# Output transposes moved one step later in the attention loop, uneven first tiles, and a regrouped layer norm in the expert stage

## What is computed

```
# attention, layer 0 (layer 1: relu projections, no bias, no time bias, no output projection)
scores = einsum('bhqd,bhkd->bhqk', Q, K) / 4          # 16 heads of 16
attn   = softmax(scores - 0.1*|t_q - t_k|)
x      = x + tanh(g) * (einsum('bhqk,bhkd->bhqd', attn, V) @ Wo.T + bo)
# feed-forward, layer 1: each row goes through the one of 4 experts that its router picks
h = gelu(x_n @ W1[e] + b1[e])                          # 256 -> 1024
y = h @ Wo + bo + x_n                                  # 1024 -> 256
y = (y - mean) * rsqrt(var + 1e-12) * gamma + beta     # over the 256 columns
x = x + tanh(g) * y
```

## Time and profile before

| | us |
|---|---|
| median of 3 runs | 765.55 |
| lowest, highest | 762.64, 770.63 |
| the profiled execution | 768.56 |
| its span, first to last instruction | 766.8 |

### The profile page before, as it was taken

How to read it: one execution, slowest core, us unless ns; L and a number is a source line. 1 busy time by engine, 2 the same in 40 slices (tenths; PEclk the granted TensorE clock), 3 DMA queues, 4 the chain that set the end, 5 groups by cost and what they waited for, 6 DMA issues and landing times.

```text
span 766.8 us, 12504 instructions
## 1 busy us (share of the span) xinstructions
PE 704.1 (92%) x4252; PEld 422.1 (55%) x4252; DVE 583.8 (76%) x1130; ACT 451.3 (59%) x968; POOL 311.2 (41%) x369
## 2 busy tenths in 40 slices
PE   6878999999999898899998999999999899999991
PEld 3434344444443566597763444444444488998981
DVE  5565899999992369455886989999997667777775
ACT  2322788888888453765414888888888234333330
POOL 4212455555554232863520020656662543443322
PEclk9998999999999999999999999999999899999997
DMA  7788645554554514102144256422301331211100
GB/s 224 213 241 192 196 151 179 190 169 153 183 187 177 165 55 113 40 1 78 39 122 111 71 169 192 140 72 84 90 2 58 100 136 45 63 45 39 48 9 23
DMA packets 51422, 87.54 MB, mean 114 GB/s; under 512 B 8661, under 2 KB 16855, under 8 KB 51360
## 3 DMA queue, kind: packets, MB, share of 16 engines
q1 hardware_dynamic: 43184, 71.39, 30.0%
q0 software_dynamic: 4640, 11.54, 5.1%
q10 hardware_dynamic: 3536, 3.81, 1.9%
HBM read 44.92 MB, written 41.63 MB: 113 GB/s over the span
## 4 chain that ended last, share of the span: by engine, by line
PE 60%; DVE 13%; POOL 10%; issue 7%; DMA 4%; SPq 3%; ACT 2%; POOLq 0%; another core or an unknown queue 0%; DVEq 0%; ACTq 0%
PE ps_out L811 10%; PE ps_wide L1004 6%; PE ps_out L1029 6%; PE ps_wide L680 6%; PE ps_a L794 6%; PE ps_a L596 5%; PE ps_misc L794 3%; PE ps_a L929 3%; POOL w_lo L1312 3%; SPq L495 2%; PE ps_a L1018 2%; PE ps_out L943 2%; DVE rows_all L1538 1%; DMA rows_all<-in_x 1%; PE ps_wide L607 1%
## 5 line engine op out<-in xcount | busy, mean ns | idle before, releaser
L1572 DVE TENSOR_REDUCE row_max<-ps_wide 128x2 f32<-128x1024 f32 x256 | 302.0, 1220 | 21.6 <-PE ps_wide L680 20.7
L1142 ACT ACTIVATE probs<-ps_a 128x512 f32<-128x512 f32 (+1 forms) x418 | 199.4, 523 | 29.9 <-PE ps_a L794 28.2
L680 PE MATMUL ps_wide<-stack_k,stack_q 48*128 48x512 f32 x512 | 145.2, 470 | 8.0 <-DVE row_max L1572 4.6
L794 PE MATMUL ps_a<-stack_q,stack_k 62*128 62x512 f32 (+3 forms) x418 | 137.9, 393 | 4.3 <-DMA stack_q<-max_rows 2.1
L811 PE MATMUL ps_out<-probs,vals 128*17 128x512 f32 x1024 | 136.7, 609 | 0.5 <-POOL probs L1372 0.5
L1142 ACT ACTIVATE probs<-ps_misc 128x512 f32<-128x512 f32 (+1 forms) x222 | 114.3, 515 | 16.4 <-PE ps_misc L794 13.8
L1372 POOL TENSOR_TENSOR probs<-probs,fixes_sb 128x512 f32<-128x512 f32 x64 | 82.2, 1284 | 92.3 <-ACT probs L1142 92.3
L794 PEld LDWEIGHTS ps_a<-stack_q,stack_k 62*128 62x128 f32 (+1 forms) x418 | 63.9, 185 | 69.7 <-ACT probs L1142 31.0
L680 PEld LDWEIGHTS ps_wide<-stack_k,stack_q 48*128 48x128 f32 x512 | 68.4, 185 | 48.4 <-DVE row_max L1572 27.5
L794 PE MATMUL ps_misc<-stack_q,stack_k 62*128 62x512 f32 (+3 forms) x222 | 87.8, 395 | 1.3 <-ACT probs L1142 1.3
L794 PEld LDWEIGHTS ps_misc<-stack_q,stack_k 62*128 62x128 f32 (+1 forms) x222 | 40.9, 184 | 39.1 <-ACT probs L1142 30.4
(11 more groups left out here) (246 smaller groups left out, 1323.8 us busy)
## 6 DMA issues: line engine op xcount, KB each, us to landing
rows_sorted<-blank SPq DMA_DIRECT2D x17, 1040.0 KB, 5.0
planes_k<-planes SPq DMA_DIRECT2D x32, 256.0 KB, 3.7
stack_k<-planes_k SPq DMA_DIRECT2D x64, 128.0 KB, 2.9
planes_q<-planes SPq DMA_DIRECT2D x32, 256.0 KB, 3.7
stack_q<-planes_q SPq DMA_DIRECT2D x64, 128.0 KB, 2.8
w_raw<-in_L_W SPq DMA_DIRECT2D x6, 1024.0 KB, 5.8
stack_k<-planes_k SPq DMA_DIRECT2D x64, 64.0 KB, 2.6
stack_q<-planes_q SPq DMA_DIRECT2D x64, 64.0 KB, 2.7
```

Of the source, the lines that this page charges most:

```text
L680: mm(raw_slot(l, ("pair", g, p))[:, i * S:(i + 1) * S], stack_q[at, slot(g, c) + q * P:slot(g, c) + (q + 1) * P], stack_k[at, slot(g, c):s ...
L794: mm(score_slot(("tile", n))[:, start:end], stack_k[at, slot(g, c) + k * P:slot(g, c) + (k + 1) * P], stack_q[at, slot(g, c) + start:slot( ...
L1142: do(probs[n % PROBS[l]][:, j, start:end], score_slot(("tile", n * TILES + t))[:, start:end], ACT.Exp, scale=0.25).then_inc(exp_done, 1)
L1572: v.tensor_reduce(row_max[:, g % 2, :, p], raw_slot(l, ("pair", g, p))[:].rearrange("p (i k) -> p i k", i=2), AX, ALU.max).then_inc(sem(f" ...
```

## The change

It does three things.

In the attention loop of both layers `turn_out` moves from the end of k = 1 to k = 2, between pieces t1 and t2, after both halves of pair p = 4. The orders of `raw_items` and of VectorE's loop follow: the output now stands before pair p = 5 (`OUT_AT`) in place of p = 4. ACT's copy of the output moves from before t0 to before t2 of k = 2.

The first head's scores are cut into 128 and 384 columns in place of 256 and 256.

In the expert stage GpSimd gets new work: gamma and beta are multiplied once by the gate (`gate_constants`), and each block's rows get the bias, and its x the gated beta, ahead of time (`prepare`). On VectorE the bias add goes, the refinement has three small steps in place of four, and the four wide steps become two. `spread` moves directly behind `residual`, `finish(n - 1)` comes in the same iteration as its `spread`, and GpSimd's loop takes root, `prepare`, `gather` and `scatter` in a new order. The residual waits for `prepared`.

```diff
+OUT_AT = PAIRS // 2 + 1
@@ raw_items, and likewise VectorE's attention loop
-                    if p == PAIRS // 2 and g >= BEHIND:
+                    if p == OUT_AT and g >= BEHIND:
@@ tile_of
-            return (0, t * S // 2, (t + 1) * S // 2) if t < 2 else (t - 1, 0, S)
+            return ((0, 0, P), (0, P, S))[t] if t < 2 else (t - 1, 0, S)
@@ TensorE, attention
                             scores(g, k, 1 + 2 * c)
                             if ahead < G and c == 0:
                                 for_maximum(l, ahead, p, 0, False)
+                            if (k, c) == (2, 0) and g >= BEHIND:
+                                turn_out(g - BEHIND)
                             scores(g, k, 2 + 2 * c)
...
                         if k == 1:
                             if g + 1 < G:
                                 turn_maximum(g + 1)
-                            if g >= BEHIND:
-                                turn_out(g - BEHIND)
@@ ACT, attention
-                            if k == 2 and t == 0 and g > 0:
+                            if k == 2 and t == 2 and g > 0:
                                 keep_out(g - 1)
@@ GpSimd, expert stage
+            def gate_constants():
+                pool.wait_ge(sem("w_last"), 16 * 7)
+                for c in (gamma, beta):
+                    v.tensor_scalar(c[:], c[:], gates[:, 3:4], None, ALU.mult).then_inc(sem("gated"), 1)
+                pool.wait_ge(sem("gated"), EARLY_ROWS * QT + 2)
+            def prepare(n):
+                pool.wait_ge(sem("rows_turned"), n + 1)
+                rows, back = sorted_rows[n % ROW_RING][:, D:2 * D], sorted_rows[n % ROW_RING][:, 0:D]
+                v.tensor_tensor(rows, rows, bias_mo[:], ALU.add).then_inc(sem("prepared"), 1)
+                v.tensor_tensor(back, back, beta[:], ALU.add).then_inc(sem("prepared"), 1)
...
+            gate_constants()
             roots(3, 3)
             for n in range(2, FIRST):
                 gather(n)
+            prepare(0)
             place_rows(2)
+            prepare(1)
+            prepare(2)
             place_rows(3)
             for n in range(3):
                 gather(FIRST + n)
             for n in range(2):
                 root4(n)
-            for n in range(2, BLOCKS + 2):
-                if n < BLOCKS:
-                    root4(n)
-                scatter(n - 2)
+            for n in range(2):
+                scatter(n)
+            for n in range(2, BLOCKS):
+                root4(n)
+                if n + 1 < BLOCKS:
+                    prepare(n + 1)
                 m = n + ROW_RING - 2
                 if FIRST + 3 <= m < BLOCKS:
                     gather(m)
+                scatter(n)
@@ VectorE, expert stage
             def residual(n):
+                dve.wait_ge(sem("prepared"), 2 * (n + 1))
                 dve.wait_ge(sem("down1_done"), n + 1)
@@ spread
-                v.tensor_tensor(rows, rows, bias_mo[:], ALU.add).then_inc(sem("biased_out"), 1)
-                dve.wait_ge(sem("biased_out"), n + 1)
@@ finish
-                v.tensor_tensor(h, r, r, ALU.mult).then_inc(st, 1)
+                v.scalar_tensor_tensor(out=h, in0=r, scalar=w, in1=r, op0=ALU.mult, op1=ALU.mult).then_inc(st, 1)
                 dve.wait_ge(st, k + 1)
-                v.tensor_tensor(h, h, w, ALU.mult).then_inc(st, 1)
+                v.tensor_scalar(h, h, -0.5, 1.5, ALU.mult, ALU.add).then_inc(st, 1)
...
-                v.tensor_scalar(rows, rows, meanvar[:, t, 0:1], y1, ALU.subtract, ALU.mult).then_inc(sem("scaled"), 1)
-                for i, (by, op) in enumerate(((gamma, ALU.mult), (beta, ALU.add))):
-                    dve.wait_ge(sem("scaled"), 3 * n + i + 1)
-                    v.tensor_tensor(rows, rows, by[:], op).then_inc(sem("scaled"), 1)
-                dve.wait_ge(sem("scaled"), 3 * n + 3)
-                v.scalar_tensor_tensor(out=back, in0=rows, scalar=gates[:, 3:4], in1=back, op0=ALU.mult, op1=ALU.add
+                v.scalar_tensor_tensor(out=rows, in0=rows, scalar=meanvar[:, t, 0:1], in1=gamma[:], op0=ALU.subtract, op1=ALU.mult
+                                       ).then_inc(sem("scaled"), 1)
...
+                v.scalar_tensor_tensor(out=back, in0=rows, scalar=y1, in1=back, op0=ALU.mult, op1=ALU.add
@@ VectorE, loop over blocks
                 residual(n - 1)
+                spread(n - 1)
                 if n < BLOCKS:
                     hidden_low(n)
...
                 if n == 3:
                     finish(0)
-                if n > 2 and n < BLOCKS:
-                    finish(n - 2)
-                spread(n - 1)
-            finish(BLOCKS - 2)
-            finish(BLOCKS - 1)
+                    finish(1)
+                if n > 2:
+                    finish(n - 1)
```

More of the change, by code:

```diff
@@ L1909, in finish @@
                 w, r, h, y1 = (z[:, t:t + 1] for z in (var_eps, root, newton, rstd))
[L1910 to L1912 removed]
+                st, k = sem("newton_step"), 4 * 4 * B + 3 * n
+                dve.wait_ge(sem("root_ready"), 4 * B + n + 1)
+                v.scalar_tensor_tensor(out=h, in0=r, scalar=w, in1=r, op0=ALU.mult, op1=ALU.mult).then_inc(st, 1)
                 dve.wait_ge(st, k + 1)
[L1914 removed]
+                v.tensor_scalar(h, h, -0.5, 1.5, ALU.mult, ALU.add).then_inc(st, 1)
                 dve.wait_ge(st, k + 2)
[L1916 removed]
+                v.tensor_tensor(y1, h, r, ALU.mult).then_inc(st, 1)
+                rows, back = sorted_rows[n % ROW_RING][:, D:2 * D], sorted_rows[n % ROW_RING][:, 0:D]
+                v.scalar_tensor_tensor(out=rows, in0=rows, scalar=meanvar[:, t, 0:1], in1=gamma[:], op0=ALU.subtract, op1=ALU.mult
+                                       ).then_inc(sem("scaled"), 1)
                 dve.wait_ge(st, k + 3)
[L1918 to L1926 removed]
+                dve.wait_ge(sem("scaled"), n + 1)
+                v.scalar_tensor_tensor(out=back, in0=rows, scalar=y1, in1=back, op0=ALU.mult, op1=ALU.add
                                        ).then_inc(sem("x_final"), 1)
```

6 lines of the change are left out of this document (removed).

## The result

| | before | after |
|---|---|---|
| device time, median of 4 runs each | 765.20 us (762.64 to 770.63) | 783.23 us (782.49 to 784.54) |
| profiled execution, its span | 768.56, 766.8 us | 783.71, 781.9 us |
| mean granted TensorE clock | 0.982 | 0.987 |

The ratio is 1.0224, 95% interval 1.0186 to 1.0262: the change costs 17 us by the ratio, 18 by the medians. 779 us was forecast, with a range of 768 to 787.

The account below looks back on a forecast made before the run. The attention loop was taken as bound by TensorE-ACT-TensorE, 2.54 us a tile. Terms: 768.56 + 18.7 - 2.0 + 0 - 4.2 + 0.6 = 781.7 us profiled, 3.0 above the median, so about 779 us, range 768 to 787.

Parts of the forecast that it names:

- The wait: Attention, groups 2 to 13: pair 5 waits for pair 4's maximum, +0.78 us a group, 24 groups, +18.7 us.
- the 0.05 allowed for t1's length: Attention: VectorE starts pair 4's maximum 0.05 us later because t1 is 128 columns longer.
- C: Attention: pair 5's wait is not exposed and the transposes hide under ACT's work; 750 us, chance 10%.
- D: Attention: pair 5's wait is exposed by half, as a later tile gives some back; about 765 us, chance 7%.
- Where there is no pair 5: Attention, groups 14 and 15 (-1.4 us) and group 1 (-0.3 twice) of the layers: together -2.0 us (0 to -3).
- The moved copy: Attention, groups 2 to 13: copying the output at t2 costs and gives nothing, covered by 1.2 us of waiting.
- The narrow tile: Attention, tiles of 128 and 384 columns: 0 us (0 to -5.7); a rival had it pay 5.7, 773 us, chance 16%.
- The tail: Expert stage, after the last matmul: 7.89 us becomes 3.51, less 0.15 allowed for `hidden_low(18)`: -4.2 us (-3.5 to -4.6).
- The start of the expert stage: Expert stage, n=3: `finish(2)` behind a root behind two scatters delays `rows_low(5)`, awaited by up(5): +0.6 us (-0.7 to 2).
- The sum: Whole kernel: 768.56 + 18.7 - 2.0 + 0 - 4.2 + 0.6 = 781.7 us for the profiled execution.
- The last step: Whole kernel: the profiled execution lies 3.0 us above the median of 765.55, so the forecast median is about 779 us.
- Rival E: Attention or expert stage: VectorE's 0.18 us of air a tile goes, or the stage stalls on `prepare`; 790 us, chance 5%.

Follow-up runs that it names:

- wide tiles: The kernel before with only the attention move (transposes, ring order, later output copy), its 256-column tiles and expert stage kept: 782.85 us, ratio 1.0217.
- the run with the expert stage alone: The changed kernel with attention and its tiles put back as before, so only the expert stage is changed: 766.36 us, ratio 0.9988.
- The maximum in two halves: The changed kernel with VectorE's maximum over pair 4 taken in two halves, each as soon as its own matmul is done: 777.67 us, ratio 1.0134.
- the run with the copy early: The changed kernel with only the output copy put back ahead of the exponentials: 784.35 us, ratio 1.0200.
- The run with the root first: Attention as before, expert stage changed, GpSimd computing block 2's root ahead of the scatters of blocks 0 and 1: 763.86 us, 0.9967; again 762.33, 0.9942.
- the thin additions: Attention as before, expert stage changed, block 2's root ahead of the scatters, `prepare`'s two additions cut from 256 columns to one: 762.64 us, ratio 0.9952.
- the copy late beside it: Attention otherwise as before, expert stage changed, block 2's root ahead of the scatters, output copy behind two exponentials: 765.66 us, ratio 0.9999.
- output behind pair 5: The changed kernel with the output transposes one place later, behind the last score of the third k tile: 782.53 us, ratio 1.0225.
- late output where free: Expert stage changed, block 2's root ahead of scatters, output copy late in all groups, transposes moved only in each layer's last two: 766.38 us, ratio 0.9991.

## Why the prediction was right, and where it was off

**The wait (+0.78 x 24 = +18.7).** Right in mechanism and size. `weigh` starts 2.99 us behind the maximum's transpose as summed, and 2.93 with wide tiles, which bears out the 0.05 allowed for t1's length too. T(2) to T(14) is 9.28 and 9.08 us longer than in the run with the expert stage alone (129.85 and 130.53), 18.4 for 24 groups. The maximum in two halves shows the link by itself. Rivals C and D are out.

**Where there is no pair 5 (-2.0).** Too large: it came to about -0.3. Group 1 gains 0.16 in each layer, not 0.3. The last two groups of layer 0 gain 0.6 (19.82 to 19.23 from T(14) to the last transposes of the output), for which 0.7 stood. But those of layer 1, for which another 0.7 stood, lose 0.6: 23.13 in after, and 22.54 or 22.55 in the four runs with unmoved transposes whose clock did not fall there. The prediction carried layer 0's rows over to layer 1, where transposes of the layer-normed rows (L717 in after) stand behind t2 in these tiles. The loss is made in group 14, whose `weigh` of k = 2 starts 3.15 us behind T(14) where it was 2.63 in the run with the expert stage alone; in layer 0 it is 1.94 for 2.21. Which wait does it was not tried.

**The moved copy (0 in groups 2 to 13).** Right here, and the reason given, that pair 5's wait covers it, is shown by the run with the copy early and by the 1.21 us between the copy's end and `weigh`. It holds only as long as that wait is there: with the transposes at their old place the same edit costs 3.3 us.

**The narrow tile (0, against -5.7).** Right: +0.03 us a group alone, +0.06 with the move (11.53 to 11.59), together 0.7 to 1.4 us over 24 groups. The reason was half right. t1 starts 0.06 earlier, so the step between the two scores is not set by a load that starts with t0; it is t1's end that doesn't come earlier. The four 128-column transposes from which the load's length was taken don't tell when it may start.

**The tail (-4.2).** Right: 7.89 to 3.67 is -4.22. `hidden_low(18)` came 0.20 later for TensorE (its last such wait is 1.27 us, before 1.07), where 0.15 was allowed. As that wait lies ahead of the last matmul, the tail's net gain is 4.22 - 0.20, so -4.0.

**The start of the expert stage (+0.6).** Here a term was mis-sized. The mechanism was named (finish(2) behind the root, behind two scatters, `rows_low(5)` behind that), but TensorE stood for 1.80 us where it didn't before, and 0.6 was reckoned, so it came out near the upper bound of 2. Two things were left out of the chain: GpSimd's issue time ahead of the second scatter (1.46 us from one scatter's start to the next, where 1.06 was reckoned), and the stretching of finish(2), whose five steps take from 662.67 to 665.03, 2.36 us for an estimate of 1.5, because `prepare(3)` runs beside them. With the clock at 1.00 the gap cost the stage 2.1 us (146.23 against 144.16). The run with the root first shows that this chain and no other made the gap.

**The sum.** 781.7 for the profiled execution against 783.71. By the table of marks the missing 2.0 are three differences. The expert stage from its first to its last matmul grew by 3.23 where 0.6 stood: +2.6, of which the clock behind the gap (0.54 for 2.6 us) can be 1.2. The stretches without a pair 5 came to -0.8 (-2.30 - 0.17 + 1.68) for -2.0: +1.2; in both the clock fell in one of the two executions and not, or elsewhere, in the other (see the last section). The stretches with a pair 5 came to 16.9 for 18.7: -1.8, mostly the group of 12.07 us in before. So part of the agreement is errors that cancel.

The last step, taking 3.0 us off because the execution of before lay so far above its median, was right about before and of no use for after, whose profiled execution lies at its median: 17 us of difference were measured, 13.1 were summed. Of these 4 us the parts measured alone give: attention 16.6 of 16.7 by the ratio, tiles 1.8 (-0.7 to 4.4) of 0, expert stage -0.9 (-3.1 to 1.3) of -3.6. Only the expert stage is clearly off its forecast; the intervals don't allow the rest to be split more finely. Rival E (790) named a stall of the expert stage, but on `prepare`; the one that came was behind the root.

## What to carry to other kernels

In a ring of n buffers used in a fixed order, count the items that one stretch of the producer puts in: the (n+1)th waits for the first's reader, so let the first be the one whose reader is short and whose start is early, and look at what is queued behind the waiting one. When an edit moves work out of a serial stretch, ask what ran in its shadow: here the copy had filled the hole that the transposes left, and moved out of it, it ended so late that the next `weigh` had to wait for it. When steps are reordered on one engine, look for a short result (a root of one column) standing behind long transfers (two scatters) that don't need it.

## What the runs showed of the hardware that was not expected

**VectorE is held by GpSimd's additions.** In the kernel after, `prepare`'s two additions run from 662.60 to 663.35 and from 663.30 to 664.02. VectorE's step of one column that starts at 662.67 ends at 663.37, with the first addition; the next one, with one tensor, takes 0.15 in the middle of the second; the third starts at 663.60 and ends at 664.05, with the second addition. The Trainium skill (SBUF — State Buffer, "SBUF: two separate sides") says that a VectorE operation with two inputs in SBUF and a GpSimd operation that reads SBUF take a common pair of ports by turns, each for its whole length. The trace agrees, and the thin additions (391 to 161 ns) bear it out. A step of 0.21 us grew to as much as 1.19 in the run with the expert stage alone (652.34), which counts when it stands ahead of a wait that matters.

**The granted clock fell behind the same gap in one execution and not in the other.** Behind the 1.8 us gap ahead of block 5 it was 0.54 in the kernel after and 1.00 in the run with the expert stage alone; of the six profiled executions that have the gap it fell there in three (after, the two maxima, the copy early). Between the layers, behind the same 1.6 and 0.7 us waits, a projection of four matmuls took 3.62 us (clock 0.55) in the execution of before and 1.98 (1.00) in that of the expert stage alone; this is 1.6 of the 2.30 us that the change seemed to gain there. It fell there in 6 of the 14 profiled executions. Windows of before and then of the run with the expert stage alone:

```profile
407.20:411.00 3.80, 3.75 (x6) 1.22 (x6) 0.48 (x1) 0.10 (x1) 0.00 (x0) 0.55 0.55 177
```

```profile
409.80:413.00 3.20, 3.18 (x8) 1.35 (x9) 1.01 (x2) 0.60 (x1) 0.00 (x0) 1.00 0.64 209
```

Around the end of attention it falls in every execution, but not in the same place. In 3 of the 14 it was on the last weighings of the attention (before, the root first, and the copy late beside it). In the other 11 these ran at 1.00, and a wait of 3.0 to 3.3 us for `normalise` followed, which doesn't arise in the first case. Behind it the clock fell in 8, after among them; in 3 (output behind pair 5, two maxima, late output where free) it stayed 1.00 there too and fell only behind a later wait of 2.3 us. First before, then after:

```profile
593.28 5.32 PE L811 MATMUL ps_out<-probs,vals 128*17 128x512 f32 x24
```

```profile
607.60 2.77 PE L812 MATMUL ps_out<-probs,vals 128*17 128x512 f32 x24
...
PE ps_wide L717 <- DVE rows_all L1726: 3.2, 1, 3.2
```

From T(14) to the first expert matmul the first case took 32.8 to 33.0 us, the second 33.8 to 34.8 in the four runs with unmoved transposes and early copy, and 34.68 in after. So most of the +1.68 of the table by marks, some 1.2 (34.2 of the run with the expert stage alone less 33.0), is this, and the rest is about what layer 1's last groups lose. Such falls are of the size of a single part of this change, so a comparison of two spans must take them out first; the table by marks shows where they lie.
